# A fused transformer block with modulated LayerNorms: the first modulation section computed straight into columns, gate rows copied by ScalarE, and PV of the first batch in another PSUM bank

## The reference

```python
mod = (silu(c) @ wmod).reshape(4, 6, 1, 512)
sa, ca, ga, sb, cb, gb = (mod[:, i] for i in range(6))
ga = sign(ga) * maximum(abs(ga), 0.25); gb = sign(gb) * maximum(abs(gb), 0.25)
h = layernorm(x) * (1 + ca) + sa
x = x + ga * attention(h, Wqkv, bqkv, Wo, bo)          # one head, d = 128
h = layernorm(x) * (1 + cb) + sb
x = x + gb * (h @ W_up.T + lora delta of the top-1 expert)
```

## Time and profile before

| | us |
|---|---|
| median of 3 runs (lowest, highest) | 181.64 (181.44, 181.71) |
| the profiled execution | 181.46 |
| its span, first to last instruction | 179.7 |
| TensorE busy | 170.8 (95%) |
| VectorE busy | 139.4 (78%) |
| ScalarE busy | 90.1 (50%) |
| GpSimd busy | 80.4 (45%) |

### The profile page before, as it was taken

The page is one execution under the profiler, slowest core; times in us unless marked ns, Lnnn a source line. Parts: engine busy times, 40 slices in busy tenths (PEclk is TensorE's granted clock), DMA queues, the critical chain, the costliest instruction groups (busy, mean ns, idle before and its releaser), DMA issues.

```text
span 179.7 us, 2828 instructions
## 1 busy us (share of the span) xinstructions
PE 170.8 (95%) x918; PEld 134.0 (75%) x918; DVE 139.4 (78%) x352; ACT 90.1 (50%) x170; POOL 80.4 (45%) x109
## 2 busy tenths in 40 slices
PE   6889999989999999999999999999999999999990
PEld 5755757878678788878867787888887878768890
DVE  1957859998969997969999839699298275989964
ACT  3375045964278894339349651713477502583100
POOL 3464201279334549041979950019694000452550
PEclk9999999999999999999999999999999999999999
DMA  4999997930041002353031753001140000001414
GB/s 160 378 387 387 387 387 145 385 106 9 0 168 71 0 2 73 96 125 122 0 117 58 201 136 75 0 0 58 60 158 22 0 2 0 0 4 58 175 48 185
DMA packets 13902, 21.32 MB, mean 119 GB/s; under 512 B 3340, under 2 KB 4112, under 8 KB 13888
## 3 DMA queue, kind: packets, MB, share of 16 engines
q1 hardware_dynamic: 13888, 21.15, 35.3%
HBM read 14.83 MB, written 4.21 MB: 106 GB/s over the span
## 4 chain that ended last, share of the span: by engine, by line
PE 68%; DVE 10%; POOL 7%; ACT 6%; issue 5%; DMA 2%; SPq 0%; POOLq 0%; DVEq 0%; ACTq 0%
PE bank L398 44%; PE bank L412 3%; PE bank L521 3%; DVE stats L1020 2%; PE bank L548 2%; DMA xs<-in_L_attn_x_dram 2%; PE bank L506 2%; ACT xn_p L845 2%; PE bank L500 2%; PE bank L572 2%; PE bank L574 2%; PE bank L503 2%; POOL rstd L1493 1%; POOL xs L1508 1%; DVE xs L1232 1%
## 5 line engine op out<-in xcount | busy, mean ns | idle before, releaser
L398 PE MATMUL bank<-wup_lo,h2hi 128*128 128x512 f32 (+1 forms) x68 | 27.3, 401 | 0.4 <-ACT h2hi L903 0.4
L884 ACT ACTIVATE xn_p<-xs,shift,rstd 128x512 f32<-128x512 f32 x16 | 13.1, 816 | 26.1 <-POOL shift L1496 26.0
L398 PE MATMUL bank<-wup_hi,h2hi 128*128 128x512 f32 (+1 forms) x68 | 25.9, 381 | 0.0
L398 PE MATMUL bank<-wup_hi,h2lo 128*128 128x512 f32 (+1 forms) x68 | 25.9, 381 | 0.0
L1493 POOL TENSOR_TENSOR rstd<-var_eps,neg_half 128x1 f32<-128x1 f32 x16 | 8.8, 552 | 37.1 <-DVE var_eps L1243 37.1
L1508 POOL TENSOR_TENSOR xs<-xs,f_gb 128x512 f32<-128x512 f32 x14 | 17.9, 1292 | 7.7 <-DVE f_gb L1297 7.7
L398 PE MATMUL bank<-h1lo,wqkv_hi 128*128 128x512 f32 x48 | 19.6, 409 | 0.7 <-DVE modT_ca L1074 0.7
L1485 POOL TENSOR_TENSOR xs<-xs,gabo 128x512 f32<-128x512 f32 x16 | 20.3, 1306 | 0.1
L398 PE MATMUL bank<-h1hi,wqkv_hi 128*128 128x512 f32 x48 | 19.0, 395 | 0.0
L398 PE MATMUL bank<-h1hi,wqkv_lo 128*128 128x512 f32 x48 | 18.9, 394 | 0.0
L1215 DVE TENSOR_TENSOR plo<-bank,phi 128x512 fp32r<-128x512 f32 x16 | 10.0, 685 | 6.7 <-ACT phi L853 6.6
(11 more groups left out here) (185 smaller groups left out, 408.7 us busy)
## 6 DMA issues: line engine op xcount, KB each, us to landing
out_dram<-xs SPq DMA_DIRECT2D x15, 256.0 KB, 2.0
stage<-in_L_wmod_dram SPq DMA_DIRECT2D x3, 1024.0 KB, 7.3
xs<-in_L_wmod_dram SPq DMA_DIRECT2D x3, 1024.0 KB, 9.5
xs<-in_L_attn_x_dram SPq DMA_DIRECT2D x3, 1024.0 KB, 7.8
stage<-xn SPq DMA_DIRECT2D x32, 64.0 KB, 2.1
xs<-in_L_attn_x_dram SPq DMA_DIRECT2D x2, 512.0 KB, 3.8
f_gb<-in_L_ffn_W_up_dram SPq DMA_DIRECT2D x1, 1024.0 KB, 11.3
gb_bc<-gates_dram SPq DMA_DIRECT2D x4, 256.0 KB, 4.2
```

The source lines that it names most:

```text
L398: mm = nc.tensor.matmul(dst, w, m, start=first and i == 0, stop=last and i == total - 1)
L884: nc.scalar.activation(xn2_p[:, t, :], xs[:, b, t, :], ACT.Identity, bias=shift[:, 1, t:t + 1], scale=rstd[:, 1, t:t + 1]).then_inc(S["xn2 ...
```

## The change

"ca" becomes a product with the blocks of "ca" as weights (128 x 128) and silu(c) (4 columns) as moving operand, summed over the contraction in PSUM, so that columns come out directly: four banks, one for each 128 features, and VectorE only adds 1. The row copies, the transposes and the warm-up products after them go. Silu moves behind all four tiles' statistics. The transposes of x tiles 2 and 3 stand between the first of the four column products and the other three. VectorE's normalisation of batch 1 is cut into three pieces around the QKV bias. The copy of the gate rows goes from VectorE to ScalarE, for "ga" after `h1_high(1)`, for "gb" after `pt_high(1)`. PV of batch 0 goes to bank 1, QKV's first part of batch 1 to bank 5, and banks 1 and 5 change roles from there on. The counts of some semaphores change with it.

```diff
 # psum_plan
-(6, "mod", 0), (7, "caT", 0), (4, "caT", 1), (4, "qkv", 0, 0), ...
+(5, "ca", 0), (7, "ca", 1), (4, "ca", 2), (6, "ca", 3), (4, "qkv", 0, 0), ...
-... (7, "x1T", 1, 3), (5, "O", 0),
+... (7, "x1T", 1, 3), (1, "O", 0),
-(1, "qkv", 1, 0), (3, "qkv", 1, 1), (0, "qkv", 1, 2),
-(5, "Y", 0, 0), ...
+(5, "qkv", 1, 0), (3, "qkv", 1, 1), (0, "qkv", 1, 2),
+(1, "Y", 0, 0), ...
-m, f = (2, 1, 3, 0, 6), (5, 7, 4)
+m, f = (2, 5, 3, 0, 6), (1, 7, 4)
 # SP
 def wait_used(g):
-    sp.wait_ge(S["mod_psum"], g + 1)
+    if g == 0:
+        sp.wait_ge(S["ca_psum"], NK)
+    else:
+        sp.wait_ge(S["mod_psum"], g)
 # TensorE
-def first_modulation_columns(half):
-    pe.wait_ge(S["mod_rows_ready"], half + 1)
-    dst = open_bank("caT", half)
-    for nt in (2 * half, 2 * half + 1):
-        mm = nc.tensor.transpose(dst[:, nt * P:(nt + 1) * P], mod_rows[:, 0, nt * P:(nt + 1) * P], ident[:])
-    mm.then_inc(S["modT_psum"], 1)
+def first_modulation_columns(nts):
+    pe.wait_ge(mod_in["ca"], 16)
+    pe.wait_ge(S["silu_step"], 4)
+    for nt in nts:
+        dst = open_bank("ca", nt)
+        for kt in range(NK):
+            mm = nc.tensor.matmul(dst[:, 0:B], raw["ca"][:, kt, nt * P:(nt + 1) * P], silu_wide[:, kt, 0:B],
+                                  start=kt == 0, stop=kt == NK - 1)
+        mm.then_inc(S["ca_psum"], 1)
 ...
 first_x1_transposes((1,))
-modulation(0)
-first_x1_transposes((2,))
-first_modulation_columns(0)
-first_x1_transposes((3,))
-first_modulation_columns(1)
-keep_warm(bank[5], 3)
+first_modulation_columns((0,))
+first_x1_transposes((2, 3))
+first_modulation_columns((1, 2, 3))
 qkv(0, (0,))
 # ScalarE, h1_high
-if b == 0 and kt % 2 == 0:
-    act.wait_ge(S["modT_ready"], 1 + kt // 2)
+if b == 0:
+    act.wait_ge(S["modT_ready"], kt + 1)
 # ScalarE
+def gate_rows_evacuate(s):
+    i = ("ga", "gb").index(s)
+    act.wait_ge(S["gate_row_psum"], i + 1)
+    nc.scalar.activation(gates[:, i, :], at("gate_row", s)[0:B, :], ACT.Copy).then_inc(S["gates_ready"], 1)
 ...
 h1_high(1, (2, 3))
+gate_rows_evacuate("ga")
 o_high(0)
 ...
 pt_high(b)
+if b == 1:
+    gate_rows_evacuate("gb")
 o_high(b)
 # VectorE
-def first_columns(half):
-    parts = at("caT", half)[:].rearrange("p (n q r) -> p n r q", n=NK, r=QUARTER)[:, :, 0:B, :]
-    nts = slice(2 * half, 2 * half + 2)
-    dve.wait_ge(S["modT_psum"], half + 1)
-    nc.vector.tensor_reduce(modT["ca"][:, nts, :], parts[:, nts], AX_X, ALU.add).then_inc(S["modT_ready"], 1)
+def first_columns(nts):
+    for nt in nts:
+        dve.wait_ge(S["ca_psum"], nt + 1)
+        nc.vector.tensor_scalar(modT["ca"][:, nt, :], at("ca", nt)[:, 0:B], 1.0, None,
+                                ALU.add).then_inc(S["modT_ready"], 1)
 ...
-ln1_stats(0, (0,)); first_ln1_aggregate(0); first_ln1_variance(0)
+for t in range(NT): ln1_stats(0, (t,)); first_ln1_aggregate(t); first_ln1_variance(t)
 (silu steps)
-for t in range(1, NT): ln1_stats(0, (t,)); first_ln1_aggregate(t); first_ln1_variance(t)
 first_ln1_normalise()
-first_modulation_rows()
-first_columns(0)
+first_columns((0, 1, 2))
 h1_low(0, (0,))
-first_columns(1)
+first_columns((3,))
 h1_low(0, (1, 2, 3))
 ...
-second_ln1_normalise()
+second_ln1_normalise((0,))
 qkv_shift_row()
+second_ln1_normalise((1, 2))
 qkv_shift()
+second_ln1_normalise((3,))
 ...
 pt_low(0)
-gate_rows_evacuate("ga")
 h1_low(1)
 ...
 pt_low(b)
-if b == 1:
-    gate_rows_evacuate("gb")
 choose_expert(b - 1)
```

More of the change, by code:

```diff
@@ L52, in psum_plan @@
     order = [
-        (5, "cT"), (0, "x1T", 0, 0), (1, "x1T", 0, 1), (2, "x1T", 0, 2), (3, "x1T", 0, 3), (6, "mod", 0),
-        (7, "caT", 0), (4, "caT", 1), (4, "qkv", 0, 0), (5, "qkv", 0, 1), (7, "qkv", 0, 2), (6, "mod", 1), (0, "modT", 1),
+        (5, "cT"), (0, "x1T", 0, 0), (1, "x1T", 0, 1), (2, "x1T", 0, 2), (3, "x1T", 0, 3),
+        (5, "ca", 0), (7, "ca", 1), (4, "ca", 2), (6, "ca", 3), (4, "qkv", 0, 0), (5, "qkv", 0, 1), (7, "qkv", 0, 2), (6, "mod", 1), (0, "modT", 1),
         (1, "qb_row"), (3, "qb_col"), (6, "mod", 2),
@@ L57, in psum_plan @@
         (7, "PT", 0, 0), (1, "PT", 0, 1), (3, "PT", 0, 2), (0, "PT", 0, 3),
[1 row of a table removed]
[1 row of a table added]
         (2, "wupT", 0), (4, "wupT", 1), (6, "wupT", 2), (7, "wupT", 3),
-        (1, "qkv", 1, 0), (3, "qkv", 1, 1), (0, "qkv", 1, 2),
-        (5, "Y", 0, 0), (4, "Y", 0, 1), (6, "Y", 0, 2), (7, "Y", 0, 3), (2, "mod", 3),
-        (5, "gateA"), (4, "loraB"), (2, "modT", 3),
-        (6, "x2T", 0, 0), (7, "x2T", 0, 1), (5, "x2T", 0, 2), (4, "x2T", 0, 3),
+        (5, "qkv", 1, 0), (3, "qkv", 1, 1), (0, "qkv", 1, 2),
+        (1, "Y", 0, 0), (4, "Y", 0, 1), (6, "Y", 0, 2), (7, "Y", 0, 3), (2, "mod", 3),
+        (1, "gateA"), (4, "loraB"), (2, "modT", 3),
+        (6, "x2T", 0, 0), (7, "x2T", 0, 1), (1, "x2T", 0, 2), (4, "x2T", 0, 3),
     ]
-    m, f = (2, 1, 3, 0, 6), (5, 7, 4)
+    m, f = (2, 5, 3, 0, 6), (1, 7, 4)
     for b in range(1, B):
@@ L209, in adaln_block @@
             const_ready silu_zero sa_zero pool_const eb_zero dve_const silu_step cT_psum
-            mod_psum mod_rows_ready modT_psum mod_sum_ready modT_ready
+            ca_psum mod_psum mod_rows_ready modT_psum mod_sum_ready modT_ready
             sa_ready sb_split_ready ga_bc_psum ga_bc_ready gate_step gate_col_ready gate_row_psum gates_ready
@@ L229, in emptied @@
             if kind == "mod":
-                return "mod_rows_ready", of[0] + 2
-            if kind == "caT":
+                return "mod_rows_ready", of[0]
+            if kind == "ca":
                 return "modT_ready", of[0] + 1
@@ L406, in modulation @@
                     pe.wait_ge(mod_in[s], 16)
-                if g == 0:
-                    pe.wait_ge(S["silu_step"], 4)
                 quarters = [(s, kt) for s in GROUPS[g] for kt in range(0, NK, len(GROUPS[g]))]
@@ L414, in modulation @@
                 mm.then_inc(S["mod_psum"], 1)
-            def first_modulation_columns(half):
-                pe.wait_ge(S["mod_rows_ready"], half + 1)
-                dst = open_bank("caT", half)
-                for nt in (2 * half, 2 * half + 1):
-                    mm = nc.tensor.transpose(dst[:, nt * P:(nt + 1) * P], mod_rows[:, 0, nt * P:(nt + 1) * P], ident[:])
-                mm.then_inc(S["modT_psum"], 1)
+            def first_modulation_columns(nts):
[7 more added lines that the diff above has]
+                    mm.then_inc(S["ca_psum"], 1)
             def modulation_columns(g):
-                pe.wait_ge(S["mod_rows_ready"], g + 2)
+                pe.wait_ge(S["mod_rows_ready"], g)
                 dst = open_bank("modT", g)
@@ L806, in modulation_rows @@
             def modulation_rows(g):
-                act.wait_ge(S["mod_psum"], g + 1)
-                if g >= 2:
-                    act.wait_ge(S["modT_psum"], g)
+                act.wait_ge(S["mod_psum"], g)
+                if g == 3:
+                    act.wait_ge(S["modT_psum"], 1)
                 nc.scalar.activation(mod_rows[:, g % 2, :], at("mod", g)[:], ACT.Copy).then_inc(S["mod_rows_ready"], 1)
@@ L893, in h2_high @@
                         else:
-                            act.wait_ge(S["modT_ready"], 3)
+                            act.wait_ge(S["modT_ready"], NK + 1)
                     nc.scalar.activation(h2hi[:, kt, :], at("x2T", b, kt)[:], ACT.Copy,
@@ L1043, in first_ln1_normalise, with second_ln1_normalise @@
                                             ALU.subtract, ALU.mult).then_inc(S["xn1_ready"], 1)
-            def second_ln1_normalise():
+            def second_ln1_normalise(tiles):
                 dve.wait_ge(S["ln1_rstd"], NT + 1)
                 dve.wait_ge(S["x1T_psum"], NK)
-                for t in range(NT):
+                for t in tiles:
                     nc.vector.tensor_scalar(xn1[:, t, :], xs[:, 1, t, :], moments[:, 0, t, 0:1], rstd[:, 0, t:t + 1],
@@ L1055, in add_parts @@
                 n, i = len(GROUPS[g]), GROUPS[g].index(s)
-                dve.wait_ge(S["modT_psum"], g + 2)
+                dve.wait_ge(S["modT_psum"], g)
                 parts = at("modT", g)[:].rearrange("p (n s q r) -> p n s r q", n=NK, s=n, r=QUARTER)[:, :, i, 0:B, :]
@@ L1083, in scale_columns @@
                                         ALU.add).then_inc(S["modT_ready"], 1)
-                dve.wait_ge(S["modT_ready"], 3)
+                dve.wait_ge(S["modT_ready"], NK + 1)
             def widen_sa():
@@ L1114, in gate_columns @@
                                                gate_tmp[:, 2, :], ALU.add, ALU.mult).then_inc(S["gate_col_ready"], 1)
[L1116 to L1119, removed]
             def qkv_shift_row():
@@ L1150, in h1_low @@
                     dve.wait_ge(S["h1_hi"], NK * b + kt + 1)
-                    if b == 0 and kt % 2 == 0:
-                        dve.wait_ge(S["modT_ready"], 1 + kt // 2)
+                    if b == 0:
+                        dve.wait_ge(S["modT_ready"], kt + 1)
                     if b >= TURNED:
@@ L1312, in _ @@
```

(7 more changed lines are left out.)

## The result

The changed kernel takes 183.66 us (median of 11 runs, 182.45 to 186.62), the kernel before 181.71 in the same session (11 runs, 181.09 to 182.41). The ratio is 1.0094, 95% interval 1.0064 to 1.0124; all ratios here leave out runs more than 1.5% above the fastest of their kernel, among them one of the kernel before at 213.32 us and two of e7 at 339 and 589 us, whose causes are open. The forecast was 181.7, no change. It is slower, by about 1.7 us, and what came is the mechanism of rival B: TensorE's clock falls.

The account below looks back on a forecast made before the run. TensorE, busy 95% of the span, was taken as the bound. Terms +0.59 (QKV start), +0.08 (LN1 pieces) and -0.59 (gate rows) sum to +0.08 us, giving 181.7 us, no change; range 180.6 to 183.4.

Parts of the forecast that it names:

- rival B: At the start up to QKV: TensorE's clock falls to 1.2 GHz, +2.3 us, 184.0; chance 0.12.
- Spacing of the narrow loads: The 32 weight loads of the "ca" columns on TensorE: 0.12 us apart, between 0.112 and 0.127.
- rival A: Narrow "ca" products are cheap, 0.079 us per load: -0.88 us in sum, 180.8; chance 0.24.
- rival C: Weight loads of the "ca" columns don't overlap, 0.19 us each: +1.7 us in sum, 183.3; chance 0.08.
- First QKV load: Start of QKV on TensorE: first load at 14.45 us instead of 13.86, counted as +0.59 us.
- PV(0): Start of PV of batch 0: old place less 0.59 plus the shift at QKV, 36.7 us.
- LayerNorm ahead of silu: First LayerNorm on VectorE: statistics 0.58 us earlier; silu ends at 9.3, hidden by the "ca" landing with 0.2 us to spare.
- "ca" at 9.49: Landing of the "ca" load at the start: 9.49 us, 7.3 us after its issue at 2.19.
- LN1 in three pieces: Batch 1's normalisation on VectorE: qkv_shift 0.26 us later, costing 0 to 0.26, taken as +0.08.
- Gate rows and PV's bank: VectorE's gate copy leaves the path to PV(0): -0.59 us; ScalarE's copy fits its idle time.
- "sb" later: SP's wait ahead of the "sb" load: met at about 14.5 us, not 10.91; hidden by the full queue, no cost.
- What holds QKV in the kernel before: Ahead of QKV's start: VectorE's h1_low, 12.88 to 13.63 us, is the last step.

Follow-up runs that it names:

- e7: e6 with silu moved behind all four tiles' statistics, modulation(0) by rows as before; 181.15 us, ratio 0.9969.
- e1: The changed kernel with 128 moving columns instead of 4 in the 32 narrow products; 181.31 us, ratio 0.9998.
- e10: e7 with batch 1's normalisation in three pieces, so all of the change but the narrow columns, with caT 1 in bank 5; 180.55 us, ratio 0.9946.
- e2: The kernel before with only the gate rows' copy on ScalarE and PV(0) in bank 1; 180.73 us, ratio 0.9967.
- e6: e2 with the second half of the transposed "ca" columns in bank 5 and the warm-ups in bank 4; 181.15 us, ratio 0.9983.
- e4: The kernel before without the three warm-up products ahead of the first QKV product; 181.51 us, ratio 0.9994.

## Why the prediction was wrong

The step that failed is the weighing of rival B: "Against it: from 30.32 to 36.66 TensorE has only transposes" at full speed. On that ground the sum has no term for the clock: every duration in it is taken at 2.4 GHz. The runs show that this term is 1.7 us: against the kernel before, the change has the ratio 1.0094 and e1, which differs from it in the width of the narrow products alone, 0.9998. The evidence was of another kind: transposes move 128 columns each, the new products 4, and e1 shows that this difference decides. It was also from another place, behind long runs of 512-column products, whereas the change took the only ones of the start, modulation(0), out; whether that mattered too no run shows. And it outweighed the case's own sign: the loads at 0.21 us apart at the start show that this start begins at 1.2 GHz. B had 0.12. That its price (+2.3, 184.0) lay close to the 183.66 measured is partly luck: the fall came in the middle of the columns, not at QKV, and lasted 6.8 us in the profiled run, not 4.7. Two of the signs of being wrong that the prediction names did appear: the first QKV load after 14.8 (15.39), and QKV products further apart than 0.23 us (4.05 / 9 = 0.45).

The Trainium skill ("TensorE: Matmul & The Clock Gate", Part 4: PE-mode transpose) holds that transposes don't count as busy for the clock. By that rule B would have been the forecast. The fall in a stretch of transposes and narrow products agrees with it; the transposes at full clock from 30.32 to 35.97 do not. In e1 the same transposes stand between wider products and the clock holds, so they do not bring the fall by themselves; no run takes them out.

By its other steps, with e1 as the sum at full clock:

- *Spacing of the narrow loads*: 0.111 us (forecast 0.12, between 0.112 and 0.127). Rival A (0.079) and rival C (0.19) fall with it. The prediction called the 72-wide products the only tiny ones of the trace; line 689 has four with 4 columns at 3.58 us, at the slow clock of the start, with loads of 128 columns on 4 partitions that stand (0.50 - 0.22) / 3 = 0.09 us apart. It would have been a point for A.
- *First QKV load*: 14.46 in e1 (forecast 14.45), 15.39 in the kernel after. The 0.93 between them: the transposes are done 0.38 later (11.96 for 11.58, since "ca" landed later and the columns began at 9.97 for 9.58), the 24 loads take 0.95 more at the fallen clock, and the 0.39 us for which e1's TensorE stood idle ahead of QKV are used up. The agreement of 14.46 with 14.45 is partly luck: the faster loads let h1_low end at 14.23 (forecast 14.40), and QKV's load came 0.23 behind it, not 0.05.
- *PV(0)*: 36.65 in e1 (forecast 36.7), and e1's ratio 0.9998 is the forecast's +0.08 us within its interval. The sum was right, for a kernel that keeps its clock and within what the interval can tell.
- *LayerNorm ahead of silu*: the last normalised tile was ready at 9.96 (forecast 9.94), silu at 9.31 (9.3), ahead of "ca": hidden. In e1 "ca" landed at 9.0 and silu, done at 9.45, was the last: the 0.2 us of cover are no more than the spread of that landing. Its columns began at 9.54, where the forecast had them, by another wait.
- *"ca" at 9.49*: it landed at 9.93. Over the profiled runs of before and after and of the experiments the same load took 6.8 to 7.9 us from its issue; the prediction took one value for fixed. This is at most half a microsecond, and a kernel before that lands late pays it too.
- *LN1 in three pieces*: forecast +0.08; the row maxima wait 0.41 us for TensorE in e1 and e10, so it has cover and costs nothing.
- *Gate rows and PV's bank*: forecast -0.59, measured -0.50 on the chain and 0.6 us in time (e2). The gate copy on ScalarE (0.57 us at 37.78 in e2) ends 0.7 us ahead of o_high, which waits for PV: in idle time, as forecast.
- *"sb" later*: issued at 15.63 (14.5 forecast, 10.91 before). In e1, which has the same wait and issues it at 14.29, no cost shows in the time.
- *What holds QKV in the kernel before*: the prediction called h1_low (to 13.63) the last step. Its chain shows VectorE's second column sum behind it, and e6, e7 and e10, with that sum in another bank, are 0.11 us quicker there.

## What to carry to other kernels

A change that replaces dense products by narrow ones in a thin stretch has a price that no duration of the old trace contains: ask first what keeps TensorE's clock up there, and take as evidence only a stretch whose products move as little, not merely one that is as busy. Where products are bound by their weight loads, wider moving operands cost nothing up to the 128 columns tried, and here they held the clock. Take a change apart: a small part of this one (the gate copy off VectorE and out of PV's bank) is worth 0.6 us alone, and everything but its headline has the lowest ratio measured, though its interval overlaps that of the small part.

## What the runs showed of the hardware

- With 128 moving columns the 24 products took 2.69 us, 0.112 each, the spacing of those with 4 columns (0.111): under a 128-column float32 weight load products of up to 128 columns were free. The Trainium skill ("TensorE: Matmul & The Clock Gate", section Back-to-back issue gap) puts the gap of 1 to 64 columns at about 25 ns, for products without their weight loads; here the load sets the spacing.
- TensorE fully busy by the profile, with products of 4 columns and transposes, lost half its clock: the mean clock is down in 11 of 11 runs, and in the profiled one it came back 4.6 us after the 512-column QKV products began (15.46 to 20.1). With 128 columns at the same spacing it fell in none of 12. In e4 TensorE stood idle from 13 to 14 us and kept 2.4 GHz.
- At the start the profile shows a granted clock of 1.00 although the loads are 0.21 us apart, the pace of 1.2 GHz. There the spacing of equal loads is the evidence, not the strip.
- The same 1 MB load, behind the same queue, landed 6.8 to 7.9 us after its issue from one profiled run to another.
